# A decoder layer in split-float matmuls: the order of the first two projection units and of the low parts that feed them

## The reference, cut to what matters

```python
x = x + attn(_layernorm(x), Wq, bq, Wk, bk, Wv, bv, Wo, bo, gq, gk)
# inside attn:
q = hidden_states @ Wq + bq
k = hidden_states @ Wk + bk
v = hidden_states @ Wv + bv
q = rms_norm(q, gq)
k = rms_norm(k, gk)
```

## Time and profile before

| what | value |
|---|---|
| median of 3 runs | 535.83 us (535.49 to 535.84) |
| the profiled execution's own time | 535.3 us |
| its span in the trace | 533.4 us |
| TensorE busy (matmul) | 521.2 us, 98% of the span |
| VectorE, ScalarE, GpSimd busy | 62%, 67%, 51% |
| chain that ended last, by engine | TensorE 92%, VectorE 4%, ScalarE 2% |

### The profile page before, as it was taken

The page is one execution under the profiler, slowest core; times in us unless marked ns, Lnnn a source line. Parts: engine busy times, 40 slices in busy tenths (PEclk is TensorE's granted clock), DMA queues, the critical chain, the costliest instruction groups (busy, mean ns, idle before and its releaser), DMA issues.

```text
span 533.4 us, 9756 instructions
## 1 busy us (share of the span) xinstructions
PE 521.2 (98%) x3221; PEld 462.8 (87%) x3221; DVE 331.5 (62%) x697; ACT 355.5 (67%) x742; POOL 270.8 (51%) x228
## 2 busy tenths in 40 slices
PE   7999999999999999999999999999999999998997
PEld 6888888878888889999999999999999999987586
DVE  6354444266666677666666666676666667666855
ACT  4666665656666767777777776776777677677730
POOL 2444444364455545654646556464655646465440
PEclk9999999999999999999999999999999999999999
DMA  5445534323333222112122111121231312120002
GB/s 183 139 138 170 203 98 169 89 79 98 98 98 98 59 82 59 49 52 60 59 59 59 51 49 57 59 59 59 59 105 58 139 60 60 60 71 29 2 0 80
DMA packets 23494, 43.42 MB, mean 81 GB/s; under 512 B 3632, under 2 KB 3888, under 8 KB 23216
## 3 DMA queue, kind: packets, MB, share of 16 engines
q1 hardware_dynamic: 23472, 43.13, 25.9%
HBM read 41.03 MB, written 2.10 MB: 81 GB/s over the span
## 4 chain that ended last, share of the span: by engine, by line
PE 92%; DVE 4%; ACT 2%; POOL 1%; issue 0%; DVEq 0%; POOLq 0%
PE p_v L612 5%; PE p_v L614 5%; PE p_o L540 5%; PE p_v L613 5%; PE p_o L541 5%; PE p_o L542 5%; PE p_t L540 5%; PE p_t L542 5%; PE p_t L541 5%; PE acc L631 5%; PE acc L632 5%; PE acc L633 5%; PE p_t L598 5%; PE p_o L650 3%; PE p_o L652 3%; PE p_o L651 3%
## 5 line engine op out<-in xcount | busy, mean ns | idle before, releaser
L1136 DVE TENSOR_TENSOR w_lo<-raw,w_hi 128x512 fp32r<-128x512 f32 x64 | 44.2, 690 | 77.0 <-ACT w_hi L743 77.0
L996 POOL TENSOR_TENSOR wo_lo<-raw,wo_hi 128x512 fp32r<-128x512 f32 x31 | 40.1, 1294 | 100.4 <-ACT wo_hi L885 100.4
L820 ACT ACTIVATE probs<-p_s,nbias,rq_t 128x256 f32<-128x256 f32 x128 | 71.3, 562 | 19.2 <-DVE nbias L1239 19.2
L743 ACT CAST w_hi<-raw 128x512 fp32r<-128x512 f32 x64 | 39.9, 623 | 62.9 <-PE p_t L542 30.3
L612 PE MATMUL p_v<-w_hi,xnt_hi 128*128 128x256 f32 x256 | 77.2, 301 | 0.0
L614 PE MATMUL p_v<-w_hi,xnt_lo 128*128 128x256 f32 x256 | 72.3, 282 | 0.0
L613 PE MATMUL p_v<-w_lo,xnt_hi 128*128 128x256 f32 x256 | 72.2, 282 | 0.0
L978 POOL TENSOR_TENSOR acc_k<-acc_k,square 128x512 f32<-128x512 f32 x32 | 41.7, 1302 | 52.9 <-ACT square L758 52.9
L978 POOL TENSOR_TENSOR acc_q<-acc_q,square 128x512 f32<-128x512 f32 x32 | 43.6, 1361 | 40.2 <-ACT square L758 39.9
L869 ACT CAST pt_hi<-p_t 128x512 fp32r<-128x512 f32 x64 | 37.4, 584 | 38.8 <-PE p_t L598 38.8
L996 POOL TENSOR_TENSOR w_lo<-raw,w_hi 128x512 fp32r<-128x512 f32 x32 | 44.9, 1402 | 20.5 <-ACT w_hi L803 20.5
(11 more groups left out here) (282 smaller groups left out, 1490.4 us busy)
## 6 DMA issues: line engine op xcount, KB each, us to landing
raw<-in_wv SPq DMA_DIRECT2D x36, 256.0 KB, 2.6
raw<-in_wk SPq DMA_DIRECT2D x32, 256.0 KB, 2.6
raw<-in_wq SPq DMA_DIRECT2D x32, 256.0 KB, 2.6
raw<-in_wo SPq DMA_DIRECT2D x31, 256.0 KB, 2.6
ctx_f<-in_ctx SPq DMA_DIRECT2D x4, 512.0 KB, 3.7
xin<-in_x SPq DMA_DIRECT2D x4, 256.0 KB, 3.3
xb<-in_x SPq DMA_DIRECT2D x4, 256.0 KB, 5.9
ctx_kept<-ctx_k SPq DMA_DIRECT2D x1, 1024.0 KB, 5.1
```

Of the source, the lines that this page charges most:

```text
L820: act.activation(probs[:, b, a, :], p_s[:, a, :], ACT.Exp, bias=nbias[:, b, a:a + 1], scale=rq_t[:, 2 * b + a:2 * b + a + 1], accum_out=rs ...
L996: pool.tensor_tensor(dst, raw[:, slot, :], hi, ALU.subtract).then_inc(w_lo_pool, 1)
```

## The change: what it does

Unit 1 no longer runs through `project`. A function `first_units` issues unit 0's passes over high x as before, then unit 1's eight matmuls over high x (into `p_flat[3]`), then unit 0's four over low x, then unit 1's four over low x. The wait for `w_lo_dve` to reach 2 stands ahead of unit 1's first matmul, and that for `xt_lo` behind its eight. On VectorE the low weights of unit 1 are made after `xnt_lo` of tiles 0 and 1 instead of after all four. Nothing is added or taken away.

```diff
-            def first_unit():
+            def first_units():
...
+                hi1, lo1 = parts(1)
+                pe.wait_ge(w_lo_dve, 2)
+                for c in range(NC):
+                    pe.matmul(p_flat[3], hi1[:, c, :], xnt_hi[:, c, :], start=(c == 0), stop=False)
+                    pe.matmul(p_flat[3], lo1[:, c, :], xnt_hi[:, c, :], start=False, stop=False)
                 pe.wait_ge(xt_lo, NT)
                 for c in range(NC):
                     mm = pe.matmul(p_flat[2], hi[:, c, :], xnt_lo[:, c, :], start=False, stop=(c == NC - 1),
                                    skip_group_check=True)
                 mm.then_inc(proj_ready, 1)
+                for c in range(NC):
+                    mm = pe.matmul(p_flat[3], hi1[:, c, :], xnt_lo[:, c, :], start=False, stop=(c == NC - 1))
+                mm.then_inc(proj_ready, 1)
...
-            for r in range(1, 4):
+            for r in range(2, 4):
                 project(0, r, 0)
...
+            weights_lo(0, 0, 0)
+            x_lo(0)
+            x_lo(1)
+            weights_lo(0, 1, 0)
+            x_lo(2)
+            x_lo(3)
+            weights_lo(0, 2, 0)
+            weights_lo(0, 3, 0)
```

More of the change, by code:

```diff
@@ L551, in sum_squares @@
                 mm.then_inc(ssq_ready, 1)
-            first_unit()
-            for r in range(1, 4):
+            first_units()
+            for r in range(2, 4):
                 project(0, r, 0)
@@ L1142, in norm_k, with x_lo @@
                                          in1=rkb[:], op0=ALU.mult, op1=ALU.mult).then_inc(k_normed, 1)
-            weights_lo(0, 0, 0)
-            for t in range(NT):
+            def x_lo(t):
                 dve.wait_ge(xt_hi if t else xt_hi_0, max(t, 1))
@@ L1149, in _ @@
                                   xnt_hi[:, :, tt], ALU.subtract).then_inc(xt_lo, 1)
-            for r in range(1, 4):
-                weights_lo(0, r, 0)
+            weights_lo(0, 0, 0)
[6 more added lines that the diff above has]
+            weights_lo(0, 3, 0)
             dve.wait_ge(const_landed, 16 * 5)
```

## The result

The changed kernel takes **536.68 us** (median of 11 runs, 536.29 to 537.01) against 535.49 us for the kernel before, timed beside it (11 runs). The ratio is 1.0022, with a 95% interval of 1.0014 to 1.0029, which is 0.75 to 1.55 us. The profiled execution took 536.49 us, with a span of 534.7.

A forecast was written before the change was run, and what follows sets the result against it. TensorE, busy 98% of the span at full clock, was taken to bound the kernel. Terms of -0.43 and +1.32 gave +0.89 us; +0.9 on the 535.83 median gave 536.7 us, 8-in-10 range 535.8 to 537.3.

The forecast's parts named there:

- Unit 1's high passes at 11.85: TensorE starts unit 1 at 11.85 on earlier low weights; 0.71 us lost before, 0.28 now, a gain of 0.43 us.
- Unit 0 complete 1.38 late, ScalarE at 14.97: Unit 0's last matmul ends at 14.86, not 13.48, so ScalarE casts unit 2's high weights only from 14.97.
- Unit 2 at 16.81, released by the square: TensorE waits from 15.61 to 16.81 for unit 0's square, 1.20 us by starts, 1.04 us idle in the profile.
- Restart cost 0.12 at unit 2: After its wait, unit 2 pays 0.12 us of restart, making the loss there +1.32 us.
- Unit 3 at 19.65 and no second wait: Unit 3 starts 12 matmuls after unit 2, at 19.65; its inputs are 1.2 us early, so the wait happens once.
- The sum: Gain of 0.43 us at unit 1 and loss of 1.32 us at unit 2: +0.89 us in all.
- D: Measure: first L518 matmul to unit 3's first, 9.05 us before. Rival: three handoffs at 0.11, +1.08 us, 536.9, chance 0.14.
- B: Rival: the old wait goes and no new one comes at unit 2; 535.4 us, chance 0.08.
- C: Rival: only the weights hold unit 2, until 16.37; sum +0.45, 536.3 us, chance 0.06.
- A: The forecast itself: a new wait at unit 2 takes the old one's place; 536.7 us, 536.3 to 537.0, chance 0.68.
- (a): Condition for unit 2's start: its low weights from VectorE, ready for TensorE at 16.37.
- E: Rival: the clock falls to 1.2 GHz behind the new wait, up to 2.72 us more; 539.4 or above, chance 0.04.

## Why the prediction was right

The mechanism that was forecast is the one in the trace: the new wait, at that place, with that releaser, of 1.14 us where 1.04 was expected, and none behind it. That the time, 536.68, lies on the 536.7 of the forecast is in part luck. The forecast added 0.9 to 535.83, the median of three runs; beside the changed kernel the old one took 535.49, 0.34 less, and the change cost 1.19 us, 0.3 more, and the two nearly cancel.

Starts below are after's less 0.25, to stand beside the prediction's.

- **Unit 1's high passes at 11.85:** 11.87, with no wait named and a restart cost of 0.11 (12.46 - 12.12 - 0.227).
- **The low parts of x hidden, unit 0's low pass at 13.79:** 13.82, no wait.
- **Unit 0 complete 1.38 late, ScalarE at 14.97:** 15.01, after 3.92 us of sleep (3.9 expected).
- **The square complete at 16.76:** 16.80 (16.37 + 0.68 - 0.25).
- **Unit 2 at 16.81, released by the square:** 16.94. This is the one term of the sum that was clearly mis-sized: the handoff from ScalarE's square to TensorE, for which no row existed. 0.05 was taken and 17.19 - 17.05 = **0.14** measured, outside the 0.03 to 0.11 that were to bound it. It repeats: 17.81 less 16.99 + 0.68 = 17.67 is 0.14 in the second profile. The trace before has ScalarE to TensorE at another place, and there it is 508.41 less 507.54 + 0.81, which is 0.06, after a wait of 1.01 us. So neither the pair of engines nor the waking from a wait makes the 0.14, and what does is not shown:

```profile
507.54 0.81 ACT L923 ACTIVATE xn<-x_res,cb,rstd 128x512 f32<-128x512 f32 x1
508.41 0.66 PE L457 MATMUL acc<-ident,xn 128*128 128x128 f32 x4 [1.01 <-ACT xn L923]
```

- **Restart cost 0.12 at unit 2:** 0.08, as unit 2 took 19.99 - 17.19 = 2.80 us instead of 2.72. This gives back a part of the handoff.
- **Unit 3 at 19.65 and no second wait:** 19.74, none. But the low weights of unit 3, forecast by 18.0, were complete at 17.58 + 1.38 - 0.25 = 18.71. The operation took 1.38 us instead of 0.69, as it stood beside GpSimd's (last section). Of the 1.2 us to spare 1.0 was left, so it cost nothing here.
- **The sum:** +0.89 forecast, +0.99 in D (the handoff +0.09, four hundredths of drift ahead of it, the restart -0.04). The timed medians say +1.19, and the interval of 0.75 to 1.55 holds both. The remaining 0.2 is not settled: it is no more than before's own D may be off, and the runs can't tell it from nothing.
- **The rivals:** B (no new wait) and C (only the weights hold unit 2) fell with the list of waits, and the run with the other bank shows that C's wait is real and stands right behind A's. Its place by before's clock is 16.99 - 0.53 = 16.46, where (a) said 16.37. D wanted all three handoffs slow: the two ahead of unit 1 were 0.03 and 0.05, as forecast, and only the third was slow, at 0.14. E did not come: the clock was at full speed around the new wait, as this row of TensorE by stretch shows (length, busy and count, granted clock):

```profile
16.00:18.00 2.00, 0.86 (x5) 1.00 0.19 16
```

- **No change or slower:** the forecast lay 0.18 us under the 0.2% that was called the edge, with a chance of 0.76 for within it and 0.22 for slower. The measured ratio, 1.0022, lies just over it, on the side that was given 0.22, and its interval of 1.0014 to 1.0029 holds the edge. The mis-sized handoff is half of that distance.

The Trainium skill's rule that TensorE can pull weight loads ahead of matmuls in flight ("TensorE: Matmul & The Clock Gate", section "Architectural detail") did not help past a wait here either. The load of L528 starts with its matmul. That of L548 starts at 17.16, 0.03 ahead of its matmul, though the low weights that its line names were complete at 16.60. It was held until the square was there:

```profile
12.12 0.19 PEld L528 LDWEIGHTS p_o<-xnt_hi,w_hi 128*128 128x128 f32 x1 [0.23 <-DVE w_lo L1144]
17.16 0.19 PEld L548 LDWEIGHTS p_t<-xnt_hi,w_hi 128*128 128x128 f32 x1 [1.53 <-DVE w_lo L1144]
```

## What to carry to other kernels

Before filling a stall with work of the next unit, look at who waits for the end of the unit that this work delays. Here 0.4 us of stall were removed. Two units on, the square had been 0.65 us early (15.38 against 16.03), and now TensorE stood still for it for 1.3 us by starts (from 14.98 + 0.91 = 15.89 to 17.19). Fill only as much as fits in the hole, and first with the pieces that need nothing made for them. A bank that is used again every second unit puts the reader of the finished bank on TensorE's path once too few matmuls stand between the end of one unit and the start of the next that writes its bank: ten left no wait here, eight left 0.23 us and four 1.14.

## What the runs showed of the hardware that was not expected

- **The clock does fall in this kernel, but elsewhere and not in every execution.** The profiled execution of the version with three matmuls ahead and the other bank took 536.77 us where its other eleven took 534.68 to 535.18. Its TensorE by stretch, late in the kernel:

```profile
508.00:510.00 2.00, 1.74 (x16) 1.00 0.00 0
510.00:512.00 2.00, 2.00 (x7) 0.53 0.00 0
512.00:514.00 2.00, 2.00 (x9) 0.62 0.00 0
514.00:516.00 2.00, 2.00 (x16) 1.00 0.00 0
```

  From about 510 to 513.5 us the clock is at the lower level, 1.2 GHz, and matmuls of 512 columns start 0.43 us apart instead of 0.23; against the median of 534.85 the execution is 1.9 us longer. Ahead of it lie 16 matmuls of one column (L450), the wait of 1.0 us at L457, and 12 matmuls of 144 columns. The same work stands in the profile of before at a clock of 1.00, so what makes it fall in one execution and not in another is not shown. The kernel before has three longer runs among 35 (537.13, 537.16 and 537.44 us, mean granted clock 0.996, 0.997 and 0.996), which look like the same kind; they have no trace. Rival E's mechanism exists, then, but not at the new wait, and it cost 1.7 us behind unit 3 where E put up to 2.72.
- **x lands at different times.** The start of L518 ranged from 9.53 to 10.58 us over ten profiled executions. This alone is wider than the effect under study. D is free of the start, but not of how VectorE's work lies to it, by 0.1 to 0.2 us (see the caution above).
- **From ScalarE's square to TensorE it takes 0.14 us** (0.14 in both profiles of the changed kernel, with half ahead and with TensorE's order alone, 0.15 in the version with four matmuls ahead: 15.21 + 0.67 = 15.88 to 16.03), against 0.06 for VectorE to TensorE (12.22 to 12.28) and 0.06 for ScalarE to TensorE at L457.
- **VectorE's low weights stand still while GpSimd adds up squares.** In the changed kernel the low weights of unit 3 start on VectorE inside GpSimd's first sum:

```profile
17.12 1.30 POOL L986 TENSOR_TENSOR acc_k<-acc_k,square 128x512 f32<-128x512 f32 x1 [8.64 <-ACT square L766]
17.58 1.38 DVE L1144 TENSOR_TENSOR w_lo<-raw,w_hi 128x512 fp32r<-128x512 f32 x1 [0.98 <-ACT w_hi L751]
```

  GpSimd ends at 18.42 and VectorE at 18.96, 0.54 later, however late it began: the same operation in the eight traces in which it starts inside such a sum takes 0.80 to 1.38 us and ends 0.54 or 0.55 us behind GpSimd. In the two in which it does not (before, and VectorE's order alone) it takes 0.69. So a change that moves two engines' work onto each other can make an operation twice as long; here it was off the path.
